# Moving the ranks one expert step on, spreading the last gates and scatters, and counting for the first table one repetition earlier, in a fused attention and mixture-of-experts kernel

## The reference

```python
q = relu(x @ Wq.T + bq); k = relu(x @ Wk.T + bk); v = x @ Wv.T + bv     # split in 16 heads
q_ = concat([q*sin, q*cos]); k_ = concat([k*sin, k*cos])
kv = einsum('nld,nlm->ndm', k_, v)
z = 1 / maximum(einsum('nld,nd->nl', q_, k_.sum(1)), 1e-4)
x = layernorm(x + (einsum('nld,ndm->nlm', q_, kv) * z) @ Wo.T + bo)
topv, topi = top_k(x @ router_w.T, 2); w = softmax(topv)
for e in range(8):
    out += gate[:, e] * (gelu(x @ w1[e].T) @ w2[e].T)
return layernorm(x + out)
```

## Time and profile before

| | |
|---|---|
| median of 3 runs | 902.43 us (900.96 to 902.84) |
| the profiled execution | 899.02 us, its span 897.2 us |
| PE busy | 805.7 us, 90% of the span |
| DVE busy | 558.5 us, 62% |
| ACT busy | 463.3 us, 52% |
| POOL busy | 426.6 us, 48% |

### The profile page before, as it was taken

One profiled execution on the slowest core, in us unless ns is written; L12 is line 12 of the kernel. 1 busy time (PEld: TensorE's weight loads), 2 busy tenths in 40 slices (PEclk: granted clock), 3 DMA queues, 4 the chain that ended last, 5 costly groups with the idle time before them and its releaser, 6 DMA issues.

```text
span 897.2 us, 22134 instructions
## 1 busy us (share of the span) xinstructions
PE 805.7 (90%) x6684; PEld 736.9 (82%) x6684; DVE 558.5 (62%) x1816; ACT 463.3 (52%) x1044; POOL 426.6 (48%) x545
## 2 busy tenths in 40 slices
PE   5998888897788987899999999998999999999990
PEld 4887878787778886788988888887999999999980
DVE  3336756776577777566666666655444457777774
ACT  4555655666566655344544444443444445666653
POOL 3885555564565565345444444453223233443442
PEclk9999999999999999999999999999999999999995
DMA  6462222232122224233323223322332264776644
GB/s 212 140 186 64 73 95 89 90 103 82 67 96 96 96 96 124 72 102 102 95 92 95 84 84 97 93 83 82 112 92 73 81 216 144 229 239 230 217 169 164
DMA packets 56467, 106.64 MB, mean 119 GB/s; under 512 B 9261, under 2 KB 37551, under 8 KB 54448
## 3 DMA queue, kind: packets, MB, share of 16 engines
q1 hardware_dynamic: 41296, 63.25, 23.4%
q0 software_dynamic: 12624, 33.84, 10.4%
q10 hardware_dynamic: 2448, 8.26, 2.4%
HBM read 61.91 MB, written 44.32 MB: 118 GB/s over the span
## 4 chain that ended last, share of the span: by engine, by line
PE 69%; DVE 11%; ACT 5%; issue 5%; another core or an unknown queue 5%; DMA 2%; SPq 1%; DVEq 0%; POOL 0%; ACTq 0%; POOLq 0%
PE PS L733 21%; PE PS L721 20%; PE PS L538 7%; PE PS L751 6%; PE PS L573 4%; PE PS L710 3%; PE PS L627 3%; DVE o L1041 2%; PE PS L596 2%; DVE o L1052 2%; PE PS L609 1%; ACT tcos L826 1%; DVE den L1050 1%; DMA xraw<-in_xT 1%
## 5 line engine op out<-in xcount | busy, mean ns | idle before, releaser
L1656 POOL DMA_INDIRECT token_rows<-xg x135 | 135.0, 1000 | 298.0 <-DVE xg L1397 273.0
L733 PEld LDWEIGHTS PS<-w,hT 128*128 128x128 f32 x1620 | 211.7, 189 | 14.0 <-issue 3.0
L721 PE MATMUL PS<-w,xgT 128*128 x810 | 222.2, 410 | 0.0
L733 PE MATMUL PS<-w,hT 128*128 x1620 | 216.5, 283 | 1.0 <-ACT hT L988 0.8
L1580 POOL DMA_INDIRECT expert_rows<-rows,idx x128 | 127.1, 993 | 93.5 <-DVE idx L1169 60.3
L721 PEld LDWEIGHTS PS<-w,xgT 128*128 128x128 f32 x810 | 143.6, 190 | 24.4 <-issue 0.2
L988 ACT ACTIVATE hT<-PS 128x512 fp32r<-128x512 f32 x135 | 80.8, 599 | 137.5 <-PE PS L751 133.2
L984 ACT ACTIVATE hg<-PS 128x512 f32<-128x512 f32 x135 | 80.7, 597 | 136.8 <-PE PS L721 120.0
L1462 DVE TENSOR_TENSOR hT<-PS,hT 128x512 fp32r<-128x512 f32 x135 | 93.4, 692 | 77.4 <-ACT hT L988 75.3
L1389 DVE TENSOR_TENSOR xgT<-PS,xgT 128x256 fp32r<-128x256 f32 x135 | 56.9, 422 | 92.9 <-ACT xgT L954 74.7
L751 PE MATMUL PS<-cst,hg 128*128 128x128 f32 x540 | 82.1, 275 | 6.0 <-ACT hg L984 3.2
(11 more groups left out here) (179 smaller groups left out, 1286.3 us busy)
## 6 DMA issues: line engine op xcount, KB each, us to landing
xg<-expert_rows SPq DMA_DIRECT2D x135, 130.0 KB
z<-token_rows SPq DMA_DIRECT2D x15, 1024.0 KB
xraw<-in_xT SPq DMA_DIRECT2D x32, 256.0 KB
xtok<-in_x SPq DMA_DIRECT2D x32, 256.0 KB
out_y<-z ACTq DMA_DIRECT2D x15, 512.0 KB, 2.9
wraw<-in_w1T SPq DMA_DIRECT2D x7, 512.0 KB, 3.7
wraw<-in_w2T SPq DMA_DIRECT2D x7, 512.0 KB, 4.2
token_rows<-xg POOLq DMA_INDIRECT x135
```

The costliest lines, as they stand in the source:

```text
L721: mm = nc.tensor.matmul(PS[:, gH, :], xgT[:, s % 2, a, k, :], w[:, bass.ds(e, 1), b, k * F:(k + 1) * F].rearrange("p o f -> p (o f)"), sta ...
L733: return nc.tensor.matmul(PS[:, gY, 0:D], hT[:, a, k, :], w[:, bass.ds(e, 1), b, HALF + k * D:HALF + (k + 1) * D] .rearrange("p o f -> p ( ...
L1656: nc.gpsimd.indirect_dma_start(yd, bass.IndirectOffsetOnAxis(ap=xg[:, XG_SLOTS[s % NXG], C_DST:C_GATE].bitcast(U32), axis=0), xg[:, XG_SLO ...
```

## The change

Five edits, none of which changes what is computed:

1. `rank` of a group moves from n = 3, behind `project_out`, to n = 4, between `hidden` and `expert`. The rank of step 4 moves likewise to step 5, and DVE's `positions` of that pair goes to step 5 with it.
2. The count for the first table: PE's `counted` moves from repetition 31 to the end of repetition 30, and DVE's `count` from `first_lengths` in repetition 31 to repetition 30, behind `positions`.
3. The `gates` of pair 31 move from n = 1 to n = 2 behind the last group, on DVE.
4. The four scatters of the pair that is ranked in step 0 go one per step into steps 1 to 4 (before: two each in steps 1 and 2).
5. The last four scatters go one per step into n = 2 to 5 (before: two each in n = 2 and 3).

```diff
@@ PE, stage 1
                 if last:
-                    counted(EARLY_PAIRS, EARLY_PAIRS - 1)
                     pe.wait_ge(table_step, 1)
@@
                 if attn:
                     attention_transposed(j, rep)
+                if rep == NPAIR - 2:
+                    counted(EARLY_PAIRS, EARLY_PAIRS - 1)
@@ PE, stage 2
                 hidden(s, now)
+                if s == 5:
+                    rank(A - 1, G - 1, A + 1)
+                if hook(s)[0] is not None and hook(s)[1] == 4:
+                    rank(hook(s)[0] - 1, LAG + hook(s)[0], hook(s)[0] + 1)
                 after = expert(s + 1) if s < STEPS - 1 else None
@@
                 if s == 4:
                     project_out(A, G - 1)
-                    rank(A - 1, G - 1, A + 1)
@@
                     if n == 3:
                         project_out(j, rep)
-                        rank(j - 1, rep, j + 1)
@@ DVE, stage 1
                 if route:
                     positions(j - 2, slot)
+                if rep == NPAIR - 2:
+                    count(0)
@@
             def first_lengths():
-                count(0)
                 made(1)
@@ DVE, stage 2
                     logits(A)
+                if s == 5:
                     positions(A - 1, 0)
-                if s == 5:
@@
                     if n == 1:
                         choose(NPAIR - 1, LAG + NPAIR, 1)
+                    if n == 2:
                         gates(NPAIR - 1, LAG + NPAIR, 1)
-                    if n == 2:
                         positions(NPAIR - 1, 1)
@@ POOL, stage 2
-                if 1 <= s <= 2:
+                if 1 <= s <= 4:
                     if s == 1:
                         scattered(A - 2)
-                    for k in range(TOPK):
-                        scatter(1, s - 1, k)
+                    scatter(1, (s - 1) // 2, (s - 1) % 2)
@@
-                    if 2 <= n < 4:
-                        scatter(1, n - 2, 0)
-                        scatter(1, n - 2, 1)
+                    if 2 <= n < 6:
+                        scatter(1, (n - 2) // 2, (n - 2) % 2)
```

## The result

| | kernel before | changed kernel |
|---|---|---|
| median of the runs | 901.69 us (900.72 to 902.84) | 886.31 us (884.83 to 887.32) |
| ratio, with 95% interval | | 0.9828 (0.9805 to 0.985) |
| profiled execution, its span | 899.02, 897.2 us | 887.25, 885.4 us |
| TensorE's mean granted clock | 0.982 | 0.975 |

The change gains 15.4 us.

The account below looks back on a forecast made before the run. PE was taken to bound a group, busy 25.1 of 26.0 us. Ranks with early scatters 7.6, gates 1.4 and count 1.2 sum to 10.2 us, from 902.43 to 892.2 us; range 888.3 to 897.2.

Parts of the forecast that it names:

- They cost nothing in sum: Early scatters: the same four, but one ahead of POOL's power in step 3 delays the next register load, -0.2 us.
- is free: Last scatters: POOL's last ends some 10 us later, near 622; SP needs them only behind the tails' stores, 639.03 to 647.
- Rival E: ACT's unexplained stop at 608 to 612.5 moves or recurs elsewhere: plus or minus 3 us, 889 to 895; chance 0.13.
- Edit 1: Nine ranks: projection's last matmul to `outputs` falls to 2.23 us each, the register load still held; gain 7.8 us.
- the row of L708: This wait executes at 398.3, when the rank starts, though its semaphores had long been raised: the register load is held too.
- The nine stretches: The nine spans from the projection's last matmul to `outputs`: 27.9 us before, 20.1 forecast.
- Edit 4 at step 5: A scatter ahead of POOL's power in step 3 delays `lsum` of step 4 by some 0.15, and step 5's register load.
- Edit 3: Last gates: PE's 1.51 us idle ahead of its transpositions goes; gain 1.4 us, bounds 0.5 and 1.5.
- Edit 2: Turn to repetition 31: PE's 1.41 us idle ahead of the projection goes; gain 1.2 us, bounds 0.5 and 1.4.
- Rival A: The register load isn't held and all edits give their most: 13.2 us, so 889.2; chance 0.17.

Follow-up runs that it names:

- a_no_scatters_2: Changed kernel with both spreadings of scatters undone, on a chip with stops: 892.73 us, 0.9898 of the kernel before.
- a_no_scatters: Changed kernel with both spreadings of scatters undone, on a chip without stops: 860.38 us, 0.9871 of the kernel before.
- b_rank: Kernel before with only the rank moved, on a chip without stops: 865.05 us, 0.9919 of the kernel before.
- a_burst_2: Changed kernel with the last four scatters all in n = 2, behind a send, on a chip with stops: 892.71 us, 0.983 of the kernel before.

## Why the prediction was wrong

**The step that failed** is the costing of the two spreadings (edits 4 and 5) at nothing: "They cost nothing in sum" and "is free". I asked what the scatters delay if they come later, and not what they hold up where they stand in a row. The right size, on a chip with stops, is a gain of 7.4 us (by the pair on chip B) to 8.4 us (alone, on chip D). With it the sum would have been 10.2 + 7.4 = 17.6, where chip B measured 17.8 (7.4, and 10.4 for the three other edits); the first set of runs, with 15.4, lies a little below that.

**The row was in hand.** Rival E named the stop of the earlier trace rows and the 2.8 us that it costs PE, and called it a thing "which nothing in the kernel explains". POOL's own timeline of the same 8 us shows the row. Rival E took the stop for a thing that moves by chance, 3 us either way, and did not ask whether an edit removes it.

**Why a stop costs more than its wait.** PE's idle time at the two stops was 2.5 and 2.8 us; the stretches gained 4.6 and 4.2. Most of the rest is the slow matmuls behind each. In the trace of before, the 3 us behind the second stop, and the whole stretch:

```profile
613.00:616.00 3.00, 2.79 (x10) 2.43 (x11) 1.83 (x4) 1.02 (x3) 0.89 (x1) 0.50 0.21 46
```

```profile
598.00:625.00 27.00, 22.18 (x144) 19.48 (x143) 14.59 (x50) 7.96 (x16) 11.35 (x13) 0.94 0.26 80
```

The granted clock is 0.50 in the 3 us behind the idle time and 0.94 in the mean of the 27 us, against 1.00 in the groups.

**Edit 1** was right in mechanism and near in size: 2.23 us forecast, 2.12 to 2.31 measured in the eight groups, in the two traces of the changed kernel. With a register load that is not held it would have been 1.96, and the row of L708 rightly stood against that: DVE's low part, which L708 waits for, had ended at 395.44 (395.02 + 0.42), and L708 executed only with the rank, 2.9 us later. The kernel before, DVE's timeline:

```profile
395.02 0.42 DVE L1389 TENSOR_TENSOR xgT<-PS,xgT 128x256 fp32r<-128x256 f32 x1
```

In the changed kernel the register load stands here:

```profile
L757 PEldq TENSOR_LOAD <-steps x1: 307/307/307, 397.2 to 397.2; - x1
```

and its first matmul of L734 at 398.04, 0.84 later. The forecast had taken 0.99, an upper bound, and a release 1.24 us behind the projection; the load starts 1.4 behind it, 0.3 behind the end of DVE's `lsum` (396.71 + 0.16), which the rank waits for. That the two errors cancel is luck. The load moved ahead of the rank gives 1.94, near the 1.96. The nine stretches gain 6.9 us (27.9 to 21.0), but the groups give back 0.16 us each outside them (23.04 us against 22.88), which leaves the 5.6. With the load first the rest of a group is 22.89 again, so the held load costs a little outside the stretch too; where, stays open.

**Edit 4 at step 5** was mis-sized. I said 0.15 to 0.2 us; it costs 0.8 on chip B. The first rank's stretch is 2.94 us there in the changed kernel and 2.18 with the scatters undone (`a_no_scatters_2`); it is 3.12 in the first trace, and 2.53 and 2.40 in `a_no_scatters` and `b_rank` on chip A. In the first trace POOL's power comes 0.6 us later than in `a_no_scatters_2`, counted from DVE's difference, DVE's low part follows it so late that PE waits 0.20 for it by itself, and DVE's `residual`, ahead of `lsum`, starts 1.25 us behind the projection's last matmul instead of 0.32; so the register load comes on top. Of the nine ranks of the changed kernel eight gained.

**Edit 3** 1.4 forecast, 1.7 in the trace, 2.0 in time. **Edit 2** 1.2 forecast, 1.6 in the trace, 3.1 (1.2 to 5.0) in time. Both held. The second table's wait, 1.4 instead of 0.5, was not forecast: in every trace without a stop at the late place it is 1.1 to 1.8 us, in the five with one it is 0 to 0.8; in the kernel before the stop had covered 0.9 of it. Something that hides a wait was taken away, and the wait came out.

**The range.** Rival A, at 889.2, was the largest gain that I could add up, and the range ended 1 us below it. An unexplained stop in a place that an edit touches should have widened it by the stops' full price, 2.5 + 2.8, to 883.

## What to carry to other kernels

When an edit moves DMAs issued by GpSimd, look not only at what waits for them but at what else stands still while they go out: lay the stops without a releaser of ACT, DVE and PE beside POOL's timeline. Here the rank's wait held up the register load behind it, which PE's sequencer executes itself: it started at 397.2, 1.4 us behind the projection's last matmul, while the array had `hidden` to run (396.04 to 397.67). Where a trace shows such a gap, put the register load ahead of the wait (here it took the nine stretches from 19.8 to 17.6 us). And the spreading, worth nothing on chips A and C (0.9998 and 1.0004), was worth 1% on chip D (0.9895), so compare only runs beside each other.

## What the runs showed of the hardware

Rows of three to six indirect DMAs of POOL (1.27 us from start to start) can stop ACT, and at times DVE, mostly for 2 to 5.6 us and mostly until 0.8 to 1.2 us behind the last one (0.5 at the late place in the trace of before); PE then waits for them, for 3.74 us at the row of five in `a_burst_2`. Pairs with a pause of 1.2 us or more behind them did not. This happens on two of the four chips here and in the first traces, in every trace with the rows of four in stage 1 (behind 12 to 15 of the 21), and on the other two chips never, with the same or longer rows. The kernel before is 29 to 36 us slower where it happens, and with the rows broken up the difference is 3 us (862.7 against 859.6).

These runs do not show what it is in the chip, or in the session, that makes a stop, nor why some rows of four pass without one. Rows of three stood only close together. The spreading also lowers the number of indirect DMAs per microsecond, and no run tells that from the pause. No trace has a record of what ACT waits for in a stop.
